# A decoder layer of attention, cross-attention and FFN on one core: the hand-written order of all five engines replaced, large weights fetched behind wq

## The chip, the core and the metric

The kernel runs on one core of a Trainium2 chip. The time is device microseconds (us) for one execution; three executions of the kernel before took 316.17, 318.11 and 319.19 us, so its median is 318.11 us. Lower is better.

## What is computed

16 sequences of 128 positions with 256 features go through three blocks. Each block is followed by a sum with its input and a layer norm without weights (`_layernorm`).

```python
# block 1: linear attention by a running sum
q, k, v = x @ Wq.T, x @ Wk.T, x @ Wv.T
x = ln(x + (q * cumsum(k * v, axis=-2) * denom) @ Wo.T)
# block 2: 32 query heads of 8 features on 8 key/value heads; keys = values = ctx_512 (16, 128, 64)
x = ln(x + softmax(x_heads @ ctx_heads.T / sqrt(8)) @ ctx_heads)
# block 3: FFN of 1024 with block quantisation over 32 values
xb = bf16(x);  h = bf16(ln(xb) * ln_w + ln_b)
h = bf16(mx_quant(h) @ mx_quant(W1).T + b1);  h = bf16(gelu(h))
h = bf16(mx_quant(h) @ mx_quant(W2).T + b2)
x = ln(x + bf16(xb + h))
```

`mx_quant` takes the largest magnitude of each 32 values, makes a power of two of it, divides, rounds and clips, and multiplies back.

## The kernel before

The 16 sequences are 8 pairs; all work is on pairs `p` = 0 to 7, with `b` = 0 or 1 for the sequence in the pair. Every engine has its own program: a `head()` that is written out, a `step(p, on)` that is repeated (`run_steps(step, 5, 9)`, four times, with `p[n]` = t - n, so that one step works on pair t-0 to t-6 in different stages), and a `tail()` written out. The engines meet only at semaphores. Each engine executes its list strictly in the order in which the calls stand, so that order is the schedule: an instruction that waits holds up all that stand behind it. The change rewrites these lists.

What each engine does, with the names used below:

- **SP** (SyncE) issues the DMAs: `load_xt` (L333 on, the transposed input), `load_x`, `load_keys`, `load_values`, `load_bias`, `load_weight(name)` for diag, wo, w1, ident, ln, tri, w2, and `store`. The ScalarE queue issues wkv (two halves) and wq at its start.
- **PE** (TensorE): `first_kv` and `kv_proj` (keys and values of block 1), `q_proj`, `running_sum` (product with a triangle), `out_proj`, `x1T` (transposes), `scores_a` (L2020, scores from which only the maximum is taken), `maxT`, `scores_b` (L2045, scores less the maximum, transposed), `weigh` (L2058), `values_back` (L2066), `weights_T`, `h_T`, `ffn_up` (L2097, L2099), `g_T` (L2111), `ffn_down` (L2122, L2124).
- **ACT** (ScalarE) copies most results out of the PSUM banks and computes `exps` (L835), `gelu` (L855), `norm1`, `norm2_x2`, `norm4`, `y2_copy` (L885), `hidden` (L849), `pv_copy` (L839). Going from Exp to Gelu and back loads a table.
- **DVE** (VectorE): `first_low`, `k_times_v` (L1220), `q_times_sum` (L1226), `residual1` (L1233), `moments` and `mean_var` (L1210, L1216), `maxima` (L1255, eight for each `p, b`, each over one `scores_a` result of 128x512), `max_high`, `max_low`, `denominators`, `attention`, `norm2`, `norm3`, and the quantisation in seven pieces: `quantise_weight(n, j, i)` for four parts of each of the two FFN weights, `quantise_h(p, i)` and `quantise_g(p, b, i)`, where i = 0 is the reduction (L1341) and 4 to 6 the wide products (L1350, L1352, L1354). For pair 7 the DVE also has `last_residual2`, `last_weight3`, `last_quantise_h` and so on, for one sequence at a time.
- **POOL** (GpSimd): `keys_rounded`, `keys` (L531), `split_xt_high` (L502), `split_xt_low` (L507), `split_bias(0..3)` (L449 to L462), `var_eps` (L481) and `rstd` (L486) of each norm, `shift_product`, `shift`, `split_x1_high`, `split_x1_low`, `residual2`, `weight3` (L568), `shift3` (L574), `ffn_out` (L580), `residual3` (L587).

The dependencies that matter below: `maxima(p,b,k)` waits for `scores_a(p,b,k)`; `scores_a` of k of 2 or more waits for the maximum two before it, since two banks are used in turn; `scores_b(p,b,k)` waits for the exponential two before it; `q_proj(p,0)` waits for `k_times_v(p,0)`; `quantise_h(p,0)` waits for POOL's `shift3(p)`, and this for DVE's `norm3`; `ffn_up` of pair 7 needs `last_quantise_h(b,6)` by way of `h_T(7,b)`; `g_T(p,b)` needs all seven pieces of `quantise_g(p,b)`.

`warm(bk, n)`, a filler of matmuls on zeros, is defined in the kernel before and called nowhere.

## Time and profile before

| | us |
|---|---|
| median of three executions | 318.11 |
| lowest, highest | 316.17, 319.19 |
| the profiled execution | 319.24 |
| its span, first to last instruction | 317.4 |
| outside the span | 1.8 |
| DVE busy in the span | 270.3 (85%) |
| PE busy | 263.5 (83%) |
| ACT busy | 223.3 (70%) |
| POOL busy | 182.8 (58%) |
| mean granted TensorE clock | 0.92 |

Times inside the profile count from the first instruction of the span. The span falls into a head up to 101.6 us, four repeated steps up to 222.7 us (found by the DVE's `maxima`, which recur every 30.2 to 30.5 us) and a tail. A row of the timeline gives start, duration, engine, line, operation, output<-input, a count where several were merged, and in brackets the idle time before it with what ended it.

### The profile page before, as it was taken

The numbers are of one execution on the slowest core, as the hardware profiler recorded it, in microseconds if no ns is written. First come the engines' busy times: TensorE is split into PE (matmuls) and PEld (weight loads), VectorE is DVE, ScalarE is ACT, GpSimd is POOL, SyncE is SP. The second block draws the span as 40 slices with busy tenths as digits, with TensorE's granted clock in tenths as the row PEclk, the third lists the DMA queues.
The fourth block names the chain that finished last, engine by engine and source line by source line (L and its number), as shares of the span: only waits on it lengthen the run. The fifth ranks groups of instructions, "written<-read, shape, count | busy, mean of one in ns | idle before, by whom it ended". The sixth has DMA issues, their size and how long they took to land. (4 is left out here: it accounts for less than half of the span.)

```text
span 317.4 us, 5160 instructions
## 1 busy us (share of the span) xinstructions
PE 263.5 (83%) x1575; PEld 164.7 (52%) x1584; DVE 270.3 (85%) x665; ACT 223.3 (70%) x364; POOL 182.8 (58%) x255
## 2 busy tenths in 40 slices
...
DMA packets 10066, 12.28 MB, mean 39 GB/s; under 512 B 2995, under 2 KB 7347, under 8 KB 9782
## 3 DMA queue, kind: packets, MB, share of 16 engines
...
q8 instruction: 13, 0.21, 0.3%
...
## 5 line engine op out<-in xcount | busy, mean ns | idle before, releaser
L1255 DVE TENSOR_REDUCE nm<-bank 128x4 f32<-128x512 f32 x128 | 84.3, 677 | 8.6 <-PE bank L2020 8.4
L835 ACT ACTIVATE p_sb<-bank 128x512 f32<-128x512 f32 x128 | 73.3, 597 | 8.9 <-PE bank L2045 7.7
L2020 PE MATMUL bank<-kbd,xT 96*128 96x512 f32 x128 | 57.6, 468 | 5.1 <-ACT xT L811 3.4
L2045 PE MATMUL bank<-xT,kbd 104*128 104x512 f32 x128 | 58.1, 466 | 4.0 <-ACT p_sb L835 2.4
L481 POOL TENSOR_SCALAR ve<-mv 128x2 f32<-128x2 f32 (+1 forms) x36 | 8.0, 221 | 63.4 <-DVE mv L1216 62.3
L531 POOL TENSOR_TENSOR kbd<-k3r,diag_sb 96x512 fp32r<-96x512 f32 x32 | 33.1, 1047 | 7.3 <-PE bank L2045 6.8
L2020 PEld LDWEIGHTS bank<-kbd,xT 96*128 96x128 f32 x128 | 25.1, 197 | 22.8 <-DVE nm L1255 12.3
L2045 PEld LDWEIGHTS bank<-xT,kbd 104*128 104x128 f32 x128 | 24.9, 196 | 21.1 <-ACT p_sb L835 14.1
L1341 DVE TENSOR_REDUCE am<-g_sb 128x32 f32<-128x1024 bf16 x16 | 30.2, 1891 | 5.2 <-ACT g_sb L855 5.2
L2058 PE MATMUL bank<-p_sb,va_sb 128*32 128x512 f32 x256 | 34.5, 631 | 0.0
L486 POOL TENSOR_TENSOR rs<-ve,nhalf 128x2 f32<-128x2 f32 (+1 forms) x36 | 27.1, 755 | 2.4
L859 ACT ACTIVATE gT<-bank 128x1024 bf16<-128x1024 bf16 x16 | 16.5, 1029 | 16.4 <-PE bank L2111 16.3
L1941 PE MATMUL bank<-wkv_r,xt_r 128*128 128x512 f32 x84 | 26.8, 452 | 0.0
L811 ACT ACTIVATE xT<-bank 96x512 fp32r<-96x512 f32 x32 | 18.9, 590 | 9.0 <-PE bank L2004 8.9
L2111 PE MATMUL bank<-idb,gq 128*128 128x128 bf16 x128 | 12.2, 252 | 14.6 <-DVE gq L1354 14.6
L849 ACT ACTIVATE y_sb<-bank 128x512 bf16<-128x512 f32 x32 | 18.9, 595 | 4.3 <-PE bank L2099 3.2
L828 ACT ACTIVATE xT<-bank 8x1024 fp32r<-8x1024 bf16 x16 | 16.2, 1015 | 6.0 <-PE bank L2033 5.5
L2124 PE MATMUL bank<-w2T,gT 128*128 128x256 bf16 x128 | 19.7, 305 | 0.0
L1210 DVE BATCH_NORM_STATS2 st<-r_sb 128x6 f32<-128x256 f32 x48 | 19.3, 415 | 0.2
L2111 PEld LDWEIGHTS bank<-idb,gq 128*128 128x128 bf16 x128 | 9.0, 113 | 19.8 <-DVE gq L1354 17.3
L1941 PEld LDWEIGHTS bank<-wkv_r,xt_r 128*128 128x128 f32 x84 | 17.1, 214 | 3.7 <-issue 0.2
L2004 PE MATMUL bank<-idr,x 128*96 128x128 f32 x128 | 17.0, 255 | 1.8 <-ACT xT L828 1.4
...
## 6 DMA issues: line engine op xcount, KB each, us to landing
xt_sb<-in_xt SPq DMA_DIRECT2D x8, 256.0 KB, 3.2
x_sb<-in_x SPq DMA_DIRECT2D x8, 256.0 KB, 3.0
out_dram<-o_sb SPq DMA_DIRECT2D x7, 256.0 KB, 2.2
...
x_all<-in_w SPq DMA_DIRECT2D x1, 1024.0 KB, 8.3
w_raw<-in_w SPq DMA_DIRECT2D x1, 1024.0 KB, 7.8
p_sb<-in_wkv ACTq DMA_DIRECT2D x2, 256.0 KB, 3.8
...
```

What stands on the lines that cost most here:

```text
L486: gp.tensor_tensor(rs[:, part(b)], ve[:, part(b)], nhalf[:, part(b)], ALU.pow).then_inc(rs_ready, batches(b))
L531: gp.tensor_tensor(kbd[0:MR, b, u, :, :], k3r[:, b, u, :].bitcast(F32).unsqueeze(1).to_broadcast([MR, KU, P]), diag_sb[0:MR, :].unsqueeze( ...
L835: sc.activation(p_sb[:, k, :], bankB[k % 2][:, :], ACT.Exp, scale=SCORE_SCALE).then_inc(s_ex, 1)
L1210: ve.bn_stats(st[:, b, :], rows).then_inc(st_ready, 1)
L1255: ve.tensor_reduce(nm[:, b, u, g, :], bankA[(2 + k + 11 * b) % 2][:, :].rearrange("p (k t) -> p k t", k=KU), AX.X, ALU.max, negate=True).t ...
L1341: last = ve.tensor_reduce(am, h.rearrange("p n i k -> p n k i"), AX.X, ALU.max, apply_absolute_value=True)
L1941: last = mm(bankP[b][:, :], xt_r[:, a, c, b, :], wkv_r[:, w, c, :], start=c == 0 and n == 0, stop=c == KC - 1 and n == len(PARTS) - 1)
L2020: mm(bankA[(2 + k + 11 * b) % 2][:, :], xT[0:MR, b, u, g, :], kbd[0:MR, b, u, :, :].rearrange("r k t -> r (k t)"), start=True, stop=True). ...
L2045: mm(bankB[k % 2][:, :], kbd[0:MR + 2 * KU, b, u, kk, :], xT[0:MR + 2 * KU, b, u, :, :].rearrange("r g s -> r (g s)"), start=True, stop=Tr ...
L2058: last = mm(value_bank(p, b)[VW * k:VW * (k + 1), :], va_sb[:, at0:at0 + VW], p_sb[:, u * KU + k, :], start=u == 0, stop=u == U - 1, tile_ ...
L2111: last = tp(dst[:, c, :], gq[:, b, c * P:(c + 1) * P], idb[:, :])
L2124: last = mm(dst, gT[:, b, c, :], w2T[:, c, :], start=False, stop=c == FC - 1)
```

## The change

No arithmetic is added or removed. All `head`, `step` and `tail` lists of SP, PE, ACT, DVE and POOL are written in a new order. Besides this:

```diff
 # load_weight, SP
+                if name in ("w1", "w2", "ln"):
+                    sp.wait_ge(s_w["wq"], 16)
                 sp.dma_start(dst, src).then_inc(s_w[name], 16)
 # split_xt_high, POOL
                 if later(p):
                     pool.wait_ge(s_qp, KC * p)
+                    pool.wait_ge(s_kvp, PB * p)
 # ffn_down, PE
-                if p == LAST:
-                    last.then_inc(s_f2, 1)
-                elif b == PB - 1:
-                    last.then_inc(s_f2, PB)
+                last.then_inc(s_f2, 1)
 # new, called nowhere
+            def warm_last(n):
+                pe.wait_ge(s_ex, 16 * NP)
+                for _ in range(n):
+                    mm(bankB[0][:, :], zero_b[:, 0:P], zero_b[:, :], start=True, stop=True)
```

So w1, w2 (1 MB each) and ln are issued only when wq has landed. The middle one fits an order in which a query projection may end before the last key/value projection. The third counts each `ffn_down` alone, so that they may stand in either order. No filler is called in either kernel.

**SP, the first loads.** Before:

```order
L340 DMA xt_sb<-in_xt 128x512
L370 DMA diag_sb<-in_diag 128x4
L370 DMA wo_sb<-in_wo 128x512
L370 DMA x_all<-in_w 128x2048
L362 DMA bias_f<-in_bias 1x1280 [waits setup_zeroed]
L362 DMA bias_f<-in_bias 1x1280 x2
L352 DMA k_sb<-in_ctx 96x512
L340 DMA xt_sb<-in_xt 128x512 [waits first_low_parts]
L357 DMA cv_sb<-in_ctxv 128x2x64
```

and now (`x_all<-in_w` is w1, `w_raw<-in_w` is w2):

```order
L340 DMA xt_sb<-in_xt 128x512
L362 DMA bias_f<-in_bias 1x1280 [waits setup_zeroed]
L362 DMA bias_f<-in_bias 1x1280 x2
L357 DMA cv_sb<-in_ctxv 128x2x64
L352 DMA k_sb<-in_ctx 96x512
L372 DMA diag_sb<-in_diag 128x4
L372 DMA tri_sb<-in_tri 128x128
L372 DMA wo_sb<-in_wo 128x512
L372 DMA x_all<-in_w 128x2048 [waits loaded_wq]
L372 DMA w_raw<-in_w 128x2048 [waits loaded_wq]
L340 DMA xt_sb<-in_xt 128x512 [waits first_low_parts]
```

The bias, the keys and the triangle moved ahead of w1, and w2 moved ahead of the second `load_xt`, of the identity and of `load_x(0)`.

**DVE, from the gelu quantisation of pair 6 to the statistics of pair 7, sequence 1.** Before, the second `attention(7,1,..)` and what follows it (`st<-r_sb` is `moments(7,1)`, the first of the chain that ends in the second FFN input of pair 7):

```order
L1282 TENSOR_TENSOR att<-bank,rden 128x4x4x8
L1350 TENSOR_TENSOR gz<-g_sb,in 128x1024
L1299 TENSOR_TENSOR r_sb<-x_all,att 128x256
L1341 TENSOR_REDUCE am<-g_sb 128x32
L1352 TENSOR_SCALAR gz<-gz 128x1024
L1344 TENSOR_SCALAR am<-am 128x32
L1346 TENSOR_SCALAR sc<-am 128x32
L1354 TENSOR_TENSOR gq<-gz,sc 128x1024
L1348 TENSOR_SCALAR in<-sc 128x32
L1350 TENSOR_TENSOR gz<-g_sb,in 128x1024
L1210 BN_STATS st<-r_sb 128x6
```

and now, where `h_sb` with 128x8 results is `last_quantise_h(0,..)`:

```order
L1279 TENSOR_TENSOR att<-bank,rden 128x4x4x8 x2
L1341 TENSOR_SCALAR am<-am 128x32
L1345 TENSOR_SCALAR in<-sc 128x8
L1296 TENSOR_TENSOR r_sb<-x_all,att 128x256
L1347 TENSOR_TENSOR z<-h_sb,in 128x256
L1207 BN_STATS st<-r_sb 128x6
L1213 BN_AGGR mv<-st 128x2
L1343 TENSOR_SCALAR sc<-am 128x32
L1338 TENSOR_REDUCE am<-g_sb 128x32
```

The statistics moved ahead of the second reduction of pair 6, and the FFN input of pair 7, sequence 0, is quantised in between.

**PE, the last FFNs.** Before, after the up-projections of pair 6 (`idb,gq` is `g_T`, `w2T,gT` `ffn_down`, `idb,hq` `h_T`, `w1T,hT` `ffn_up`):

```order
L2111 MATMUL bank<-idb,gq 128x128 x16
L2122 MATMUL bank<-bias_h,ones_b 128x256
L2124 MATMUL bank<-w2T,gT 128x256 x8
L2122 MATMUL bank<-bias_h,ones_b 128x256
L2124 MATMUL bank<-w2T,gT 128x256 x8
L2081 MATMUL bank<-idb,hq 128x128 x4
L2097 MATMUL bank<-bias_h,ones_b 128x512
L2099 MATMUL bank<-w1T,hT 128x512 x2
```

and now:

```order
L2081 MATMUL bank<-idb,hq 128x128 x2
L2097 MATMUL bank<-bias_h,ones_b 128x512
L2099 MATMUL bank<-w1T,hT 128x512 x2
L2111 MATMUL bank<-idb,gq 128x128 x8
L2097 MATMUL bank<-bias_h,ones_b 128x512
L2099 MATMUL bank<-w1T,hT 128x512 x2
L2111 MATMUL bank<-idb,gq 128x128 x8
L2122 MATMUL bank<-bias_h,ones_b 128x256
L2124 MATMUL bank<-w2T,gT 128x256 x8
L2081 MATMUL bank<-idb,hq 128x128 x2
L2122 MATMUL bank<-bias_h,ones_b 128x256
L2124 MATMUL bank<-w2T,gT 128x256 x8
```

Sequence 0 of pair 7 is projected up before pair 6 is projected down; sequence 1 follows between the two down-projections.

Other moves that are spoken of below, as lines of the diff:

```diff
 # POOL head
+                split_bias(0)
+                split_bias(1)
                 keys_rounded(0)
...
 # DVE head
                 first_low(3)
+                k_times_v(0, 0)
                 quantise_weight(0, 3, 0)
...
 # PE step: the first calls now
+                    kv_proj(p[1], 0, 0)
+                    kv_proj(p[1], 0, 1)
+                    scores_b(p[3], 0, 0)
+                    scores_b(p[3], 0, 1)
+                    x1T(p[3], 1, 1)
+                    kv_proj(p[1], 1, 0)
+                    q_proj(p[1], 0)
+                    kv_proj(p[1], 1, 1)
                     scores_b(p[3], 0, 2)
                     scores_a(p[3], 1, 0)
...
 # PE tail: the scores of pair 6 now end ahead of weigh(6, 0, 0)
+                scores_a(6, 1, 6)
+                scores_a(6, 1, 7)
                 scores_b(6, 0, 6)
                 scores_b(6, 0, 7)
+                g_T(4, 1)
                 weigh(6, 0, 0)
...
 # PE tail: and those of pair 7, sequence 0, ahead of weigh(6, 1, 0)
+                scores_a(7, 0, 6)
+                scores_a(7, 0, 7)
+                ffn_up(5, 1, 0)
+                weigh(6, 1, 0)
...
 # ACT tail
                 maxT(7, 1)
+                norm2_x2(6, 0)
+                norm2_x2(6, 1)
+                exps(7, 1, 0)
                 y2_copy(5)
-                exps(7, 1, 0)
...
 # POOL tail
+                ffn_out(5)
                 var_eps(7, mv2, ve2, s_mv2, s_ve2, 0)
                 rstd(7, ve2, rs2, s_ve2, s_rs2, 0)
+                residual3(5)
                 var_eps(7, mv3, ve3, s_mv3, s_ve3, 0)
-                ffn_out(5)
-                residual3(5)
                 rstd(7, ve3, rs3, s_ve3, s_rs3, 0)
```

## Rows read from the trace of the kernel before

**Rows 1.** The page's first part: busy time of the two busiest engines.

```profile
PE 263.5 (83%) x1575; PEld 164.7 (52%) x1584; DVE 270.3 (85%) x665; ACT 223.3 (70%) x364; POOL 182.8 (58%) x255
```

**Rows 2.** By stretch: length, busy PE, PEld, DVE, ACT, POOL, clock, DMA share, GB/s.

```profile
28.20:60.00 31.80, 27.52 (x148) 19.02 (x149) 30.01 (x68) 14.13 (x27) 20.74 (x23) 0.95 0.11 32
60.00:101.60 41.60, 38.69 (x240) 23.26 (x239) 37.69 (x93) 33.42 (x54) 28.49 (x36) 1.00 0.13 40
...
162.30:192.50 30.20, 29.15 (x196) 19.01 (x195) 28.91 (x72) 27.59 (x46) 21.81 (x31) 1.00 0.13 36
...
222.70:246.90 24.20, 22.58 (x116) 11.62 (x117) 16.97 (x41) 17.86 (x33) 14.57 (x18) 0.80 0.03 12
246.90:266.30 19.40, 14.83 (x83) 7.45 (x83) 17.96 (x44) 17.00 (x25) 8.33 (x14) 0.91 0.04 14
...
280.40:293.70 13.30, 6.48 (x36) 4.16 (x36) 12.02 (x39) 2.70 (x4) 3.38 (x8) 0.50 0.00 1
293.70:317.40 23.70, 9.79 (x47) 5.53 (x48) 11.68 (x29) 10.00 (x17) 5.09 (x10) 0.64 0.10 35
```

**Rows 3.** Timeline of the DVE, head: first reductions, stalls, first maximum.

```profile
10.40 3.04 DVE L1341 TENSOR_REDUCE wam<-x_all 128x16 f32<-128x512 f32 x3 [1.65 <-DMA x_all<-in_w]
...
15.24 2.42 DVE L1346 TENSOR_SCALAR wsc<-wam 128x16 bf16<-128x16 f32 x1
...
20.33 0.17 DVE L1346 TENSOR_SCALAR wsc<-wam 128x16 bf16<-128x16 f32 x1
...
24.93 0.42 DVE L1220 TENSOR_TENSOR kv_sb<-bank,v_sb 128x256 f32<-128x256 f32 x1 [1.36 <-ACT v_sb L816]
...
28.23 0.69 DVE L1255 TENSOR_REDUCE nm<-bank 128x4 f32<-128x512 f32 x1
```

**Rows 4.** Timeline of POOL, head.

```profile
15.15 1.26 POOL L449 TENSOR_SCALAR bias_h<-bias_f 96x1280 bf16<-96x1280 f32 x1
16.37 1.26 POOL L507 TENSOR_TENSOR xt_r<-xt_sb,xt_r 128x512 fp32r<-128x512 f32 x1
...
29.33 2.62 POOL L451 TENSOR_TENSOR bias_rest<-bias_f,bias_h 96x1280 f32<-96x1280 f32 x1
```

**Rows 5.** DMA issues: size, median us from issue to landing.

```profile
x_all<-in_w SPq DMA_DIRECT2D x1, 1024.0 KB, 8.3
...
p_sb<-in_wq ACTq DMA_DIRECT2D x1, 256.0 KB, 5.7
```

**Rows 6.** Timeline of the DVE, tail: the waits, and one late statistic.

```profile
231.23 0.69 DVE L1255 TENSOR_REDUCE nm<-bank 128x4 f32<-128x512 f32 x1 [1.48 <-PE bank L2020]
...
237.00 0.69 DVE L1341 TENSOR_REDUCE am<-h_sb 128x16 f32<-128x512 bf16 x1 [2.78 <-POOL h_sb L574]
...
245.27 0.69 DVE L1255 TENSOR_REDUCE nm<-bank 128x4 f32<-128x512 f32 x1 [1.12 <-PE bank L2020]
...
276.42 0.41 DVE L1293 TENSOR_SCALAR h_sb<-xb_all,mv,rs 128x256 f32<-128x256 bf16 x1 [3.44 <-POOL rs L486]
...
280.82 0.41 DVE L1299 TENSOR_TENSOR r_sb<-x_all,att 128x256 f32<-128x256 f32 x1
...
284.96 0.42 DVE L1210 BATCH_NORM_STATS2 st<-r_sb 128x6 f32<-128x256 f32 x1
...
298.93 1.87 DVE L1341 TENSOR_REDUCE am<-g_sb 128x32 f32<-128x1024 bf16 x1 [5.20 <-ACT g_sb L855]
```

**Rows 7.** Timeline of PE, tail: one `weigh`, the last `g_T` and `ffn_down`.

```profile
228.53 1.94 PE L2058 MATMUL bank<-p_sb,va_sb 128*32 128x512 f32 x8
...
232.47 1.07 PE L2058 MATMUL bank<-p_sb,va_sb 128*32 128x512 f32 x8
...
290.81 1.91 PE L2124 MATMUL bank<-w2T,gT 128*128 128x256 bf16 x8
...
306.95 1.04 PE L2111 MATMUL bank<-idb,gq 128*128 128x128 bf16 x8 [0.23 <-DVE gq L1354]
```

**Rows 8.** Timeline of ACT: issue of wq, and both `norm2_x2(6)` where they stood.

```profile
1.64 0.45 ACTq L779 DMA_DIRECT2D p_sb<-in_wq  x1
...
262.91 1.08 ACT L869 ACTIVATE x_all<-r_sb,nb,rs 128x256 f32<-128x256 f32 x2
```

More of the change, by code:

```diff
@@ L1030, in step @@
                 if on[4]:
-                    hidden(p[4], 0, 0)
-                    norm2_x2(p[4], 1)
+                    hidden(p[4], 0, 1)
                 if on[3]:
@@ new lines, in head @@
+                moments(1, 1, r1_sb[:, 1, :], st1, s_r1, 2 * 1 + 2, s_st1)
+                maxima(0, 1, 0)
+                quantise_weight(1, 0, 3)
+                quantise_weight(1, 2, 3)
+                quantise_weight(1, 1, 1)
+                quantise_weight(1, 3, 3)
+                maxima(0, 1, 1)
+                mean_var(1, 1, st1, mv1, s_st1, s_mv1)
+                maxima(0, 1, 2)
+                k_times_v(2, 0)
+                maxima(0, 1, 3)
+                quantise_weight(0, 0, 3)
@@ new lines, in head @@
+                quantise_weight(1, 1, 4)
+                moments(0, 0, r2_sb[:, 0, :], st2, s_r2, 2 * 0 + 1, s_st2)
+                moments(0, 1, r2_sb[:, 1, :], st2, s_r2, 2 * 0 + 2, s_st2)
+                maxima(1, 1, 0)
+                mean_var(0, 0, st2, mv2, s_st2, s_mv2)
+                maxima(1, 1, 1)
+                maxima(1, 1, 2)
+                mean_var(0, 1, st2, mv2, s_st2, s_mv2)
+                quantise_weight(1, 3, 5)
+                quantise_weight(1, 1, 5)
+                k_times_v(3, 1)
@@ new lines, in tail @@
+                quantise_g(6, 0, 0)
+                denominators(7, 1)
+                attention(7, 1, 0)
+                attention(7, 1, 1)
+                quantise_g(6, 0, 1)
+                last_quantise_h(0, 3)
+                last_residual2(1)
+                last_quantise_h(0, 4)
+                moments(7, 1, r2_sb[:, 1, :], st2, s_r2, 2 * 7 + 2, s_st2)
+                mean_var(7, 1, st2, mv2, s_st2, s_mv2)
+                quantise_g(6, 0, 2)
+                quantise_g(6, 1, 0)
@@ L2341, in step @@
                 if on[3]:
[L2342 removed]
                     scores_a(p[3], 1, 7)
+                    weigh(p[3], 0, 1)
                 if on[5]:
```

1027 lines of the change are left out of this document (483 added, 544 removed).

## Prediction
> **What bounds the kernel now.** I read the page's busy times first. DVE is busy 270.3 of 317.4 us and PE 263.5 [rows 1], so neither is hidden behind another engine and DVE leaves 47.1 us idle in all. No instruction is added or removed on either, so a new order can only buy idle time back or make more of it. The reader should therefore look for where those 47 us lie, and the table by stretch shows it [rows 2]. In one repeated step DVE is busy 28.91 of 30.20 us and PE 29.15: 1.3 and 1.05 us free. From 28.2 to 60.0 us DVE has 1.8 us free, from 60.0 to 101.6 us 3.9. In the tail it is different: 24.20 - 16.97 = 7.2 us free up to 246.9, 1.4 up to 266.3, 1.3 from 280.4 to 293.7 and 23.70 - 11.68 = 12.0 at the end. Then I read the timeline of the DVE at the two ends for what ended each wait [rows 3, 6], and that of POOL, PE and ACT beside it [rows 4, 7, 8]. So the middle is bound by DVE's own work with PE close behind, and the ends by waits. Times are worked out against the profiled execution: 319.24 us, a span of 317.4 and 1.8 around it. It lies 1.1 us above the median of 318.11, and I take that off at the end.
>
> **Head, up to the first maximum.** DVE starts the first `maxima` at 28.23 us. Before it stand three losses [rows 3]: 1.65 us until w1 lands, 2.42 us for a tiny scalar piece that elsewhere takes 0.17 (so 2.25 lost), and 1.36 us until a copy of ACT. The long piece lies exactly over POOL's `split_bias(0)` and `split_xt_low(1)`, which run from 15.15 to 17.63 us, and ends at 17.66 [rows 4].
> The new order issues bias and keys first, so POOL can do both bias splits before 10 us; nothing small of the DVE stands there any more, and I count the 2.25 us as gone. The 1.36 us wait goes too: `kv_proj(1)` waited on PE behind `out_proj(0,1)`, which comes earlier since `k_times_v(0,0)` no longer stands behind three weight reductions (3.04 us).
> Against this stands the new wait for wq. wq was issued at 1.64 us [rows 8] and took 5.7 us [rows 5], so it landed at 7.3; w1 took 8.3 from its issue, sharing the queues. If both stay as slow, w1 lands at 7.3 + 8.3 = 15.6 us, 5.2 later than before, and all DVE reductions with it. The other bound is no delay at all: the same megabytes move, wq no longer shares with w1, and w1 no longer with wkv. I take w1 at 11 us, 0.6 late, nearer the second bound, since total bytes bind; `k_times_v(0,0)` is done meanwhile. Queued behind the waiting DMA on SP are w2, the second `xt`, the identity and x(0); the identity is used late, the others I expect by 15 us, before their users. So -2.25 - 1.36 + 0.6 = -3.0, and 0.5 less for what is late next (q and running sum on PE): **-2.5 us**, between -4.5 and +2.
>
> What could spoil it is that POOL's bias splits, 1.26 and 2.62 us long [rows 4], now run while DVE makes the low parts of wkv and wq, on which the first projections wait. Rows 3 and 4 show one DVE instruction held until POOL is done, but of another kind.
> The Trainium skill, "SBUF — State Buffer", section "Who interferes with whom", says that a vector instruction with two SBUF inputs contends with a GpSimd one that reads SBUF, and that the one that starts first has the shared ports for its whole length. By that rule those subtractions would be held as well, and this part of the change speaks against itself; the held piece agrees with the exclusive lock, and no row here shows it for a subtraction.
>
> **Steps and the later head, 28.2 to 222.7 us.** The order of PE at the start of a step now puts all of `kv_proj` and `q_proj(p,0)` ahead of `scores_a(p,1,0)`. Is it late? From the last `maxT` on, 8 + 12 + 6 + 3 + 4 = 33 matmuls stand ahead of it (19 before). At 29.15/196 = 0.149 us each [rows 2] that is 4.9 us (2.8). DVE now has 18 instructions between `max_low(p,0)` and `maxima(p,1,0)` (12 before), at 28.91/72 = 0.40 us each 7.2 us (4.8). So the margin is 2.3 us against 2.0: still hidden. The same holds for POOL's `weight3` and `shift3`, whose place in the chain is the same, so their short wait stays. DVE work is equal, so a step cannot fall under 28.9 us: at most -1.3 us for each of four steps, and I see nothing that would add more than 1. I take **+0.5 us** for the whole stretch, for small waits in the 42 + 32 us of head with its weight pieces in another order; bounds -5 and +5. If the margin is used up, every further us on PE costs one per step.
>
> **Tail, by the waits of rows 6.**
> - `scores_a(6,1,6)` and `(6,1,7)` stood behind `weigh(6,0,0)`, which took 1.94 us there against 1.07 at the other clock [rows 7]; DVE waited 1.48 us. They now stand ahead: -1.5.
> - `scores_a(7,0,6)` and the next stood behind `weigh(6,1,..)`; DVE waited 1.12 us at 245.27. Now ahead: -1.0.
> - The wait of 2.78 us at 237.00 for POOL stays: `quantise_h(5)` has nothing new before it.
> - ACT now does both `norm2_x2(6)`, 1.08 us [rows 8], between `maxT(7,1)` and the exponentials of the last sequence, where they used to fill a gap; with `y2_copy` behind two split down-projections I count +1.3.
> - POOL no longer has `residual3(5)` in front of `rstd` of sequence 0 of pair 7, so most of the 3.44 us wait at 276.42 goes. That by itself buys nothing, since the second sequence still waits for its exponentials; it makes room to quantise sequence 0 early. 0.
> - From the end of `attention(7,1)` to the last `last_quantise_h`, DVE has 39 instructions in 13.30 us, 12.02 busy, 0.31 each [rows 2]; `moments(7,1)` came 284.96 - 281.23 = 3.7 us after its input [rows 6]. Now 34 stand there and the statistics follow at once: 5 x 0.31 = 1.5, less 0.4 for a chain with less between its links: -1.1.
> - The end. DVE waited 5.20 us for the gelu and then did both quantisations, 298.93 to 306.95 us [rows 6, 7], 8.0 us or 4.0 each. Now sequence 0 is quantised in the gap. The gelu of sequence 1 stays about 7.4 us behind `last_quantise_h(1,6)`: it loses the wait for sequence 0 and gains `ffn_down(6,1)`, 1.91 us [rows 7]. Then 4.0 us: `g_T(7,1)` can start 11.5 us after 293.7 instead of 13.2. `ffn_down(7,0)` is no longer behind `g_T(7,1)`, worth 0.2 more: -1.9. Cover gone: if `ffn_down(6,1)` delays the gelu by all of its 1.91 us, this term is 0.
>
> Tail: -1.5 - 1.0 + 1.3 - 1.1 - 1.9 = **-4.2 us**, between -8 and +1.
>
> **Sum.** -2.5 + 0.5 - 4.2 = -6.2 us: 313.0 on the scale of the profiled execution, **311.9 us** as a median.
>
> **Rivals.**
> 1. *The ends give little.* w1 comes 3 us late or POOL holds the low parts by its 1.26 + 2.62 us, and `ffn_down(6,1)` takes the last term away. Head +1 instead of -2.5, tail -2.3: 318.1 + 1 + 0.5 - 2.3 = 317.3; with the tail part alone 313.8, with the head part alone 315.4. For it: neither the landing nor such a hold is in the trace. Against it: 12 us of free DVE at the end are there to be used.
> 2. *More is won.* If the steps give back half of their 1.3 us and the 7.2 us of the first tail stretch are halved, that is another -2.6 - 1.1: 308. For it: the free time is there. Against it: in the steps PE is nearly full as well.
> 3. *Slower: the granted clock.* PE has 1.05 us free per step, at clock 1.00. Where `kv_proj` and `q_proj` are missing, the clock was 0.80 over a stretch [rows 2] and `weigh` took 1.94 instead of 1.07 us. `q_proj(p,0)` now stands early and waits for `k_times_v(p,0)`, with the scores behind it; if these pauses let the clock fall, PE decides from 29.15/30.2 = 0.965 down. At 0.90 a step takes 32.4 us, 2.2 more, over some 5.4 steps (162.7 us from 60.0 to 222.7) 11.9: 323.8 us. Against it: all steps before ran at 1.00 with pauses of their own, and the matmuls are as many.
> That the change does not do what it says is no rival: the order on each engine is fixed by the lists.
>
> **How the numbers follow.** My forecast 0.52, rival 1 0.22, rival 2 0.11, rival 3 and unseen waits in the steps 0.15. About 1% (3.2 us) is what a measurement of this kernel can tell from no change. The forecast and rival 2 are faster by more, 0.63; of rival 1 most lies within 1%, with a little of rival 3: 0.21; the rest, 0.16, slower. The range takes in rival 2's side (307.0) and, upward, rival 1 and the beginning of rival 3 (319.5).
>
> **What would show it.** Right: the first `maxima` at 25 to 26.5 us, no scalar piece of 2.4 us near 15 us, step length 29.8 to 30.5 us by the distance of equal `maxima`, clock 1.00 in the steps, the wait of 5.20 us before the first gelu reduction of pair 7 split into two short ones, and 22 us instead of 23.7 from the last `last_quantise_h` to the end. Wrong: `first_low` pieces of more than 1 us beside a bias split, w1 reductions that begin after 12 us, or steps over 31 us with PE waiting ahead of `q_proj`.

## The result, and the profile after

The changed kernel took 329.17 us (median of four executions, 327.76 to 330.04), the kernel before 318.65 us beside it on the same chip: ratio 1.033, interval 1.026 to 1.041. It is slower by 10.5 us, where I had forecast 6.2 us faster; the time lies outside my range as well. The profiled execution after took 330.04 us with a span of 328.2. In the ratios of this document executions more than 1.5% above the fastest of their kernel are left out; in e3_tail (below) one execution of 311.86 us stands so far under the other three (316.72 to 319.11) that no ratio is left.

The page of the changed kernel, busy times and granted clock (one digit per 8.2 us, in tenths of full speed):

```profile
PE 270.9 (83%) x1584; PEld 169.9 (52%) x1584; DVE 277.3 (85%) x665; ACT 221.5 (67%) x364; POOL 184.8 (56%) x255
...
PEclk9987799879999999999999999999568985895675
```

DVE does the same 665 instructions as in [rows 1] and is busy 7.0 us longer, PE 7.4 us. So the loss is not only waiting, of which the DVE has 3.8 us more (50.9 for 47.1): the same instructions took longer. To find where, I cut both spans at the same work: the first `maxima`, and then `max_high(p,b)`, which closes the eight maxima of a sequence. Both tables by stretch have the columns length, busy PE, PEld, DVE, ACT, POOL, clock, DMA share, GB/s. Cuts: first maximum, `max_high(0,0)`, `(1,1)`, `(2,1)`, `(6,0)`, end. The kernel before:

```profile
28.20:36.40 8.20, 5.87 (x23) 3.76 (x23) 8.17 (x16) 0.51 (x2) 6.97 (x8) 1.00 0.03 5
36.40:77.80 41.40, 38.35 (x224) 25.18 (x224) 37.98 (x93) 26.54 (x47) 28.30 (x35) 0.96 0.14 43
77.80:111.40 33.60, 31.67 (x212) 20.28 (x217) 31.25 (x77) 28.79 (x47) 20.53 (x28) 1.00 0.08 25
111.40:216.80 105.40, 102.22 (x678) 66.15 (x675) 100.65 (x243) 96.06 (x157) 79.08 (x107) 1.00 0.10 29
216.80:317.40 100.60, 67.94 (x371) 35.72 (x372) 73.56 (x198) 64.43 (x101) 37.64 (x61) 0.78 0.04 14
```

and after:

```profile
26.30:38.10 11.80, 9.80 (x29) 6.47 (x29) 9.73 (x14) 0.00 (x0) 6.11 (x6) 0.71 0.02 3
38.10:85.70 47.60, 38.78 (x225) 25.28 (x225) 41.63 (x102) 25.58 (x46) 26.94 (x33) 0.93 0.13 39
85.70:119.10 33.40, 30.58 (x204) 18.72 (x201) 30.36 (x71) 28.76 (x46) 20.35 (x27) 1.00 0.09 25
119.10:226.40 107.30, 102.96 (x688) 67.55 (x684) 100.85 (x243) 94.90 (x158) 77.49 (x105) 1.00 0.09 28
226.40:328.20 101.80, 72.23 (x375) 38.93 (x373) 76.66 (x199) 64.89 (x102) 38.32 (x64) 0.72 0.04 14
```

The account: up to the first maximum -1.9; to `max_high(0,0)` +3.6; to `(1,1)` +6.2; to `(2,1)` -0.2; the steps +1.9; the tail +1.2. The sum is +10.8, the difference of the spans. Nine tenths of it lie between 26 and 86 us, in the stretch for which I had allowed half a microsecond. Of the 6.2, 3.65 are busy time of the DVE. This is the DVE there, after:

```profile
54.19 0.28 DVE L1349 TENSOR_SCALAR wqb<-wz 128x512 bf16<-128x512 int16 x1
...
55.00 3.39 DVE L1349 TENSOR_SCALAR wqb<-wz 128x512 bf16<-128x512 int16 x2
...
58.91 1.22 DVE L1343 TENSOR_SCALAR wsc<-wam 128x16 bf16<-128x16 f32 x1
60.04 0.68 DVE L1252 TENSOR_REDUCE nm<-bank 128x4 f32<-128x512 f32 x1
60.64 1.02 DVE L1349 TENSOR_SCALAR wqb<-wz 128x512 bf16<-128x512 int16 x1
```

and POOL in the same microseconds, `split_bias(3)`:

```profile
55.57 2.67 POOL L456 TENSOR_TENSOR bias_low<-bias_rest,bias_mid 96x1280 bf16<-96x1280 f32 x1
58.40 1.71 POOL L460 TENSOR_SCALAR bias_h<-bias_mid 32x1280 bf16<-32x1280 bf16 x1 [0.16 <-POOL bias_low L456]
60.26 1.25 POOL L463 TENSOR_SCALAR bias_h<-bias_low 32x1280 bf16<-32x1280 bf16 x1 [0.15 <-POOL bias_h L460]
```

A cast takes 0.28 us when alone and two take 3.39 beside `bias_low`; each long piece ends within 0.2 us of the end of POOL's instruction. I call such a piece held. The maximum at 60.04, which reads a PSUM bank, keeps its 0.68. Adding up what pieces took over their usual time, where that is more than 0.3 us, the stretch from `max_high(0,0)` to `(1,1)` has 3.3 us of it before and 6.9 after. Between the first maximum and `max_high(0,0)` there is none before, and after there are three, which usually take 0.69, 0.17 and 0.17 us, 2.4 over in all:

```profile
26.90 1.27 DVE L1347 TENSOR_TENSOR wz<-x_all,win 128x512 int16<-128x512 f32 x1
28.10 1.00 DVE L1341 TENSOR_SCALAR wam<-wam 128x16 uint32<-128x16 uint32 x1
...
31.79 1.14 DVE L1341 TENSOR_SCALAR wam<-wam 128x16 uint32<-128x16 uint32 x1
```

And PE from 28 us on, after:

```profile
29.75 1.39 PE L2020 MATMUL bank<-kbd,xT 96*128 96x512 f32 x2 [1.32 <-DVE nm L1252]
31.33 0.80 PE L2020 MATMUL bank<-kbd,xT 96*128 96x512 f32 x1 [0.19 <-DVE nm L1252]
31.93 3.78 PE L1980 MATMUL bank<-wo_sb,vh_sb 128*128 128x256 f32 x8
```

`out_proj(1)` took 1.99 us before. PE had paused 1.32 us (28.43 to 29.75) for a maximum that stood behind two held pieces; the granted clock was 1.00 up to 29.4 us and at its lower level from there to 36.3 (0.50 from 31 to 35 us, where the kernel before has 1.00); and `residual1(1)`, now ahead of two maxima, waited 1.77 us for the product.

### The profile page after: what moved, and what is told of

It reads as the page before. It is cut to its first block, busy times and chain, and to the rows that moved or that the text cites. A ratio compares the mean times of both kernels' runs of the same rounds, so it can differ in the third digit from the quotient of the medians.

```text
span 328.2 us, 5176 instructions
## 1 busy us (share of the span) xinstructions
PE 270.9 (83%) x1584; PEld 169.9 (52%) x1584; DVE 277.3 (85%) x665; ACT 221.5 (67%) x364; POOL 184.8 (56%) x255
## 3 DMA queue, kind: packets, MB, share of 16 engines
q1 hardware_dynamic: 9606, 11.16, 10.5%
## 4 chain that ended last, share of the span: by engine, by line
PE 42%; DVE 34%; issue 10%; ACT 8%; DMA 3%; POOL 2%; ACTq 0%; POOLq 0%; DVEq 0%
DVE nm L1252 7%; PE bank L2020 7%; PE bank L2058 6%; PE bank L2045 5%; DVE am L1338 5%; PE bank L1980 5%; PE bank L2124 4%; PE bank L2099 3%; DVE st L1207 3%; DVE gz L1347 2%; PE bank L1941 2%; DVE xb_all L1285 2%; PE bank L2097 2%; DVE gq L1351 2%; DMA x_all<-in_w 2%
## 5 line engine op out<-in xcount | busy, mean ns | idle before, releaser
L835 ACT ACTIVATE p_sb<-bank 128x512 f32<-128x512 f32 x128 | 72.1, 602 | 22.2 <-PE bank L2045 21.5
L2020 PE MATMUL bank<-kbd,xT 96*128 96x512 f32 x128 | 63.2, 514 | 12.3 <-DVE nm L1252 7.8
L2045 PE MATMUL bank<-xT,kbd 104*128 104x512 f32 x128 | 55.2, 467 | 7.4 <-ACT p_sb L835 5.3
L533 POOL TENSOR_TENSOR kbd<-k3r,diag_sb 96x512 fp32r<-96x512 f32 x32 | 33.6, 1066 | 23.7 <-PE bank L2045 23.6
L2020 PEld LDWEIGHTS bank<-kbd,xT 96*128 96x128 f32 x128 | 26.8, 210 | 34.8 <-DVE nm L1252 21.6
L2058 PE MATMUL bank<-p_sb,va_sb 128*32 128x512 f32 x256 | 35.3, 648 | 0.0
L1338 DVE TENSOR_REDUCE am<-g_sb 128x32 f32<-128x1024 bf16 x16 | 30.5, 1906 | 3.0 <-ACT g_sb L855 3.0
L1941 PE MATMUL bank<-wkv_r,xt_r 128*128 128x512 f32 x84 | 26.0, 431 | 0.0
L859 ACT ACTIVATE gT<-bank 128x1024 bf16<-128x1024 bf16 x16 | 16.4, 1024 | 10.8 <-PE bank L2111 10.8
L1980 PE MATMUL bank<-wo_sb,vh_sb 128*128 128x256 f32 x64 | 19.5, 439 | 0.6 <-DVE vh_sb L1223 0.6
L2099 PE MATMUL bank<-w1T,hT 128*128 128x512 bf16 x64 | 20.0, 395 | 0.0
L582 POOL TENSOR_TENSOR s_sb<-y_sb,xb_all 128x512 bf16<-128x512 bf16 x7 | 8.1, 1156 | 18.2 <-ACT y_sb L885 18.2
L1941 PEld LDWEIGHTS bank<-wkv_r,xt_r 128*128 128x128 f32 x84 | 16.3, 208 | 3.1 <-issue 0.3
```

The costliest lines, as they stand in the source:

```text
L533: gp.tensor_tensor(kbd[0:MR, b, u, :, :], k3r[:, b, u, :].bitcast(F32).unsqueeze(1).to_broadcast([MR, KU, P]), diag_sb[0:MR, :].unsqueeze( ...
L835: sc.activation(p_sb[:, k, :], bankB[k % 2][:, :], ACT.Exp, scale=SCORE_SCALE).then_inc(s_ex, 1)
L1338: last = ve.tensor_reduce(am, h.rearrange("p n i k -> p n k i"), AX.X, ALU.max, apply_absolute_value=True)
L1941: last = mm(bankP[b][:, :], xt_r[:, a, c, b, :], wkv_r[:, w, c, :], start=c == 0 and n == 0, stop=c == KC - 1 and n == len(PARTS) - 1)
L1980: last = mm(out_bank(p, b)[:, b * D:(b + 1) * D], vh_sb[:, e, b, :], wo_sb[:, e, :], start=e == 0, stop=e == KC - 1)
L2020: mm(bankA[(2 + k + 11 * b) % 2][:, :], xT[0:MR, b, u, g, :], kbd[0:MR, b, u, :, :].rearrange("r k t -> r (k t)"), start=True, stop=True). ...
```

## The experiments

In the mixed kernels a part (head, step or tail) is taken on all engines from one kernel and the rest from the other. Where only one order is mixed in, the last 11 to 24 calls of each head belong to the step, since the two orders can't be joined elsewhere; such a seam costs something of its own, which I give. Ratios are to the kernel before, on the same chip. The table holds, from one profiled execution each, the lengths of the account above: A first maximum to `max_high(0,0)`, B to `(1,1)`, C to `(2,1)`, step (mean of three, `(3,0)` to `(6,0)`), tail (`(6,0)` to the end).

| kernel | span | A | B | C | step | tail | ratio, interval |
|---|---|---|---|---|---|---|---|
| before | 317.4 | 8.1 | 41.5 | 33.5 | 30.21 | 100.6 | |
| after | 328.2 | 11.8 | 47.6 | 33.4 | 30.82 | 101.8 | 1.033, 1.026 to 1.041 |
| e1_head | 326.8 | 11.6 | 46.6 | 36.6 | 30.28 | 101.5 | 1.037, 1.029 to 1.045 |
| e2_step | 324.7 | 8.1 | 41.5 | 35.6 | 30.83 | 103.5 | 1.023, 1.011 to 1.036 |
| e3_tail | 316.5 | 8.1 | 41.5 | 33.6 | 30.30 | 99.0 | see there |
| e4_loads | 319.4 | 8.1 | 41.5 | 33.6 | 30.29 | 100.8 | 1.006, 1.001 to 1.011 |
| e5_step_qcopy | 323.0 | 8.1 | 41.5 | 35.5 | 30.75 | 103.6 | 1.025, 1.019 to 1.030 |
| e6_tail_mix | 314.7 | 8.1 | 40.7 | 33.6 | 30.31 | 98.4 | 0.992, 0.987 to 0.997 |
| e7_head_bias_early | 323.7 | 12.0 | 43.2 | 36.6 | 30.31 | 100.7 | 1.025, 1.021 to 1.030 |
| e8_head_pieces_late | 324.5 | 11.4 | 44.6 | 36.4 | 30.30 | 100.7 | 1.028, 1.021 to 1.036 |
| e9_head_three | 327.0 | 12.2 | 44.8 | 36.5 | 30.28 | 100.8 | 1.035, 1.029 to 1.042 |
| e10_step_pool | 325.4 | 8.1 | 41.5 | 35.1 | 30.82 | 103.7 | 1.024, 1.019 to 1.030 |
| e11_head_filler | 326.9 | 9.7 | 46.7 | 36.6 | 30.29 | 100.9 | 1.035, 1.028 to 1.042 |
| e12_best | 321.4 | 10.2 | 40.0 | 33.6 | 30.28 | 101.0 | 1.012, 1.006 to 1.018 |
| e13_step_two | 326.8 | 8.1 | 40.6 | 38.9 | 30.48 | 103.2 | 1.014, 1.006 to 1.023 |
| e14_filler_first | 324.0 | 9.7 | 46.6 | 36.4 | 30.30 | 100.6 | 1.028, 1.020 to 1.037 |
| e15_head_first_pieces | 328.7 | 12.5 | 43.4 | 37.8 | 30.29 | 102.0 | 1.025, 1.013 to 1.037 |
| e16_after_four | 319.4 | 11.9 | 43.2 | 33.4 | 30.46 | 99.1 | 1.010, 1.005 to 1.015 |

The profiled executions of e13 and e15 were the longest of their four, so their spans lie higher than their ratios. A of the old head is 8.1 in all eight kernels that have it, and the old step 30.2 to 30.3, so 0.2 us can be read in these. B of the old head is 41.5 in six kernels and 40.6 and 40.7 in e13 and e6, where the clock was 1.00 all through it for 0.96 in the others, so in B only more than 1 us can be read. The start of the first maximum can't be read from one pair: it lies between 27.3 and 29.8 us in the seven kernels with the old lists up to there and between 24.9 and 27.4 in the nine with the new ones, 28.5 and 26.0 on average. Nor can the tail: the same new tail took 101.8 in the changed kernel and 99.0 and 99.1 in e3 and e16, at different clocks, told below.

**One part alone.** e1, e2, e3: one of head, step, tail is new. e4: the SP's head list and the wait for wq are new.

```diff
 # e4
+                if name in ("w1", "w2", "ln"):
+                    sp.wait_ge(s_w["wq"], 16)
```

> The kernel before with the new head of all engines (with the wait for wq), its own repeated step and tail; the last 11 to 24 calls of each head, which prepare the first step, stay as in the kernel before. Theory A (the loss was made in the head after the first maximum, where the DVE's weight pieces and POOL's bias pieces now stand otherwise): first maximum near 26.3 us, maxima(2,1,1) near 110 us instead of 103.4, steps of 30.2 us, median 7 to 8 us over the kernel before, ratio 1.02 to 1.025. Theory B (the whole order is denser, the granted clock falls by its total and each part alone costs little): maxima(2,1,1) within 2 us of 103.4 and a ratio under 1.01.

> The kernel before with the new repeated step alone (and the last calls of each head, which prepare it). Theory A: each of the four steps 0.6 us longer because of its own order: 30.8 instead of 30.2 us between equal maxima, median +2.4 us, ratio about 1.008. Theory B: the longer steps were a consequence of the state in which the new head left the engines: 30.2 us per step, ratio 1.00.

> The kernel before with the new tail alone. By my prediction's tail sum -4.2 us (ratio 0.987). By what the changed kernel's milestones say (+1.4 from maxima(6,1,1) to the last maximum, -0.6 after it): +0.8 us, ratio 1.003. Theory B (the clock of 0.71 to 0.76 in that stretch instead of 0.83 to 0.90 was left over from the slower steps before): then the tail alone shows 0.83 to 0.90 again and gains 2 us or more, ratio 0.994 or less.

> The kernel before with the new order of the SP's loads and the wait for wq alone, all other lists as before. Theory A (loads do no harm): w1 reductions of the DVE start at 11 to 12 us instead of 10.40, first maximum at 28.2 to 29.5, ratio 0.998 to 1.004. Rival (the loads bring w2, x or the second xt late and so cause the later loss): maxima(2,1,1) 3 us or more after 103.4 and ratio 1.01 or more.

The head alone is as slow as the whole change (329.48 us against 319.51). It starts the first maximum at 24.9 us, the earliest of all, and loses that and much more in A and B. Its C, 3.1 too long, is the seam: in the changed kernel C is no longer than before. Theory B of e1, that only the whole is slow, has fallen. The step alone is 0.62 us longer per step, as in the changed kernel; e2's seam costs 2.1 in C. Its tail is 2.9 longer, but 1.9 of that lies between `max_high(7,0)` and `(7,1)` at a clock of 0.65 for 0.90, and the same list took as long there (19.0 to 19.3 us) in e1, e11 and e15: that part is the clock and not the seam. e3: medians 317.51 against 319.51 us, a gain of 1.6 in the tail by the table, less than the 4.2 I had summed and more than the changed kernel shows. Between `max_high(6,1)` and `(7,1)` its clock was 0.97 and 0.83, where the changed kernel had 0.80 and 0.75, which is theory B's way. e4: the loads change no later length, so they are not the loss. Its first maximum is at 29.7 us, but e10, with the old loads, has 29.8, so a delay by the loads isn't shown.

**The head: held pieces.** e7 moves one POOL call into a gap of 10.9 us, e8 moves DVE pieces (and `attention(0,0,1)` behind `maxima(1,0,1)`), e9 does both and one thing more.

```diff
 # e7, POOL head
                 split_bias(2)
+                split_bias(3)
...
                 split_xt_low(3)
-                split_bias(3)
```

```diff
 # e8, DVE head; e9: this, e7 and residual1(1) behind maxima(0,0,7)
-                quantise_weight(1, 3, 4)
-                quantise_weight(1, 1, 2)
                 maxima(1, 0, 0)
-                quantise_weight(1, 0, 5)
-                quantise_weight(0, 1, 6)
...
                 maxima(1, 0, 4)
+                quantise_weight(1, 3, 4)
+                quantise_weight(1, 1, 2)
                 maxima(1, 0, 5)
+                quantise_weight(1, 0, 5)
                 maxima(1, 0, 6)
+                quantise_weight(0, 1, 6)
```

> As e1_head, with one edit: POOL's split_bias(3) (bias_low 2.66 us, then 1.71 and 1.25) stands right behind split_bias(2), where POOL idles 10.9 us from 31.5 us on, and no longer beside the weight pieces of the DVE at 54 to 60 us. Theory A1 (these pieces were held by POOL: two of 0.28 us took 3.38, one of 0.17 took 1.23, one of 0.28 took 1.02, 4.6 us in all): the held pieces vanish there, and the median falls by 3 to 5 us under e1_head. Theory A2 (the order of the DVE starves PE, the held pieces are a detail): they vanish, but the median falls by less than 1.5 us.

> As e1_head, with one edit: four weight pieces of the DVE that stood between max_low(0,1) and maxima(1,0,1) stand behind maxima(1,0,4) to (1,0,6), and the second half of attention(0,0) behind maxima(1,0,1). Theory A2 (PE waits for maxima held back by weight pieces, its clock falls to half, and the rest of the head runs late): maxima(1,0,1) 2 us or more earlier, clock in 50 to 70 us above the 0.81 of e1_head, median 3 us or more under e1_head. Theory A1: the pieces held by POOL only move; median within 1.5 us of e1_head.

> As e1_head, with three edits together: the bias edit of e7, the four weight pieces of e8, and residual1(1) behind maxima(0,0,7) again, as in the kernel before. Spans so far: e1_head 326.8, e7 323.7, e8 324.5. If the held pieces and the starved PE are two separate losses: span near 320.5 (326.8 - 3.1 - 2.3 - 1 for the residual's wait), max_high(2,0) near 98 us, median ratio 1.01. If both edits attack the same microseconds (the DVE's stretch from 53 to 60 us): span 323 or more, no better than e7 alone.

The same pieces of the DVE in e7:

```profile
54.41 0.96 DVE L1358 TENSOR_SCALAR wqb<-wz 128x512 bf16<-128x512 int16 x2
55.30 0.68 DVE L1356 TENSOR_TENSOR wz<-w_raw,win 128x512 int16<-128x512 f32 x1
55.90 0.16 DVE L1352 TENSOR_SCALAR wsc<-wam 128x16 bf16<-128x16 f32 x1
58.04 0.69 DVE L1261 TENSOR_REDUCE nm<-bank 128x4 f32<-128x512 f32 x1 [1.98 <-PE bank L2033]
```

0.96 for 3.39 and 0.16 for 1.22 us. B falls by 3.4 us. The median falls by 3.3, from 10.0 to 8.0 us over that of the kernel before on the same chip, and the ratio from 1.037 to 1.025: theory A1, at the low end of its range or below it. The clock is not what e7 gained: e11, without this edit, had the same mean clock in B (0.96) and took 46.7. The gain is not larger, since of the 4.2 us freed here (2.43, 1.06 and, at 60.64, 0.74) 1.98 come back as a wait for PE. e8 gains 2.0 in B, between the two theories, but e9 with both is no better than e8 and no better than e7 (44.8, 44.6 and 43.2). A separate loss by a starved PE, as A2 said, should have shown in e9 on top of e7's gain, and it did not: that theory has no support left. Where e8's 2.0 come from is open. Its two casts beside `bias_low` still take 3.39 us, and the moved pieces are held again where they stand now (1.09 us for two of 0.17, 1.12 for one of 0.28); its clock in B was 1.00 for e1's 0.93. Putting `residual1(1)` back bought nothing while `out_proj(1)` still ran slow (A 12.2).

**The head: the clock.** e11 and e14 put matmuls on zeros, whose results are thrown away, into pauses of PE.

```diff
 # e11, PE head
+                warm(bankB[0], 8)
                 maxT(0, 1)
 # e14, PE head
+                warm(bankB[0], 2)
                 scores_a(0, 0, 2)
                 running_sum(1)
+                warm(bankB[0], 5)
                 scores_a(0, 0, 3)
                 scores_a(0, 0, 4)
+                warm(bankB[0], 1)
                 scores_a(0, 0, 5)
+                warm(bankB[0], 1)
                 out_proj(1, 0)
```

> As e1_head, with eight matmuls of zeros on PE ahead of maxT(0,1), where it idles 2.45 us (they are thrown away). The granted clock was 0.81 from 50.5 to 68.8 us in e1_head. Theory clock (the pause lets TensorE's clock fall and this sets the time after it): the matmuls after 52.8 us run at full speed, clock 0.9 or more there, max_high(1,0) 1.5 us or more earlier than 68.8, median lower by as much. Theory A (the DVE's pieces are the bound there): PE is faster, but max_high(1,0) moves by less than 0.5 us.

> As e1_head, with nine matmuls of zeros on PE between scores_a(0,0,2) and out_proj(1), in pauses of 0.35 to 1.22 us (thrown away). In all kernels with the new head the granted clock is 0.50 somewhere between 27 and 35 us, where the kernel before has 1.00, and out_proj(1) takes 3.5 to 3.6 us instead of 1.99. Theory clock: with the pauses filled the clock stays at 1.00, out_proj(1) takes 2.0 us, max_high(0,0) comes 1.5 to 2 us earlier counted from the first maximum (9.7 instead of 11.6), and the median falls by 1 to 2 us. Theory A: out_proj is faster, but the DVE's held pieces still set max_high(0,0): under 0.7 us.

PE in e14, with the fillers from L1918:

```profile
26.94 1.24 PE L1918 MATMUL bank<-zero_b 128*128 128x512 bf16 x5
28.41 1.09 PE L2033 MATMUL bank<-kbd,xT 96*128 96x512 f32 x2 [0.23 <-DVE nm L1261]
29.34 0.39 PE L1918 MATMUL bank<-zero_b 128*128 128x512 bf16 x1
29.70 0.50 PE L2033 MATMUL bank<-kbd,xT 96*128 96x512 f32 x1
30.04 0.39 PE L1918 MATMUL bank<-zero_b 128*128 128x512 bf16 x1
30.30 1.99 PE L1993 MATMUL bank<-wo_sb,vh_sb 128*128 128x256 f32 x8
```

`out_proj(1)` takes 1.99 us again, the clock is 1.00 from 27 to 35 us, and A falls from 11.6 to 9.7, just the 1.9 that the clock theory said. The median is 2.3 us under e1's, but the intervals of the ratios overlap. In e11 the clock of the filler's stretch was 0.91 for 0.81 and B did not move (46.7): there the held pieces set the pace and a faster PE waits. But e11's A is 9.7 too, with no filler there: its clock stayed at 1.00 from 27 to 35 us after a pause of PE of 1.31 us. And in e1 the clock was at its lower level from 26.8 us on, before the pause of 1.22 us at 27.18. So what is shown is the price of the lower clock, 1.9 us in A and nothing in B of this head. That the pauses bring it on and that the fillers keep it off is not shown: without them it stayed up once (e11) and fell five times (the changed kernel, e1, e7, e8, e9), with them it stayed up in the one profile there is.

> As e7_head_bias_early, with one more edit on the DVE: the two weight pieces between maxima(0,0,0) and maxima(0,0,1), which were held by POOL (1.27 for 0.91 and 1.00 for 0.17 us), stand behind maxima(0,0,3). Theory A: PE's pause there goes, its clock stays up, max_high(0,0) 10 us or less after the first maximum instead of 12.0, median 1.5 to 2.5 us under e7. Rival: the pieces are needed by something else at once or are held where they stand now: within 0.7 us of e7.

e15 is e7 with `quantise_weight(0,1,4)` and `(0,0,1)` behind `maxima(0,0,3)`. A is 12.5: the rival was right. Both are held again where they stand now (1.24 and 0.72 us), and `x_all<-r_sb` takes 1.77 instead of 0.41 us beside the moved `bias_low`. (That piece takes 1.77 us in e7 already.) A's other 1.6 us (9.7 against 8.1) fit the three held pieces shown above, 2.4 us over their usual time, but no run took them away, so that is argued.

**The step.** e5 and e13 change ScalarE's list, e10 takes POOL's step from the kernel before.

```diff
 # e5, ACT step; e13 does both
+                    q_copy(p[1])
                     pv_copy(p[3], 0)
-                    q_copy(p[1])
 # e13, ACT step
                     hidden(p[4], 0, 0)
+                    norm2_x2(p[4], 1)
...
                     hidden(p[4], 1, 1)
-                    norm2_x2(p[4], 1)
                     gelu(p[4], 1)
```

> As e2_step (new repeated step alone), with one edit: ScalarE's q_copy(p[1]) stands ahead of pv_copy(p[3], 0) again. Theory A (the step's own loss is that q_copy waits behind pv_copy for weigh, and the DVE's q_times_sum for q_copy: 0.83 to 0.93 us in each step of e2_step): the wait of the DVE for q_sb goes and a step is 30.0 to 30.2 us again, median 2.5 to 3.5 us under e2_step. Rival (PE's new order at the start of the step, with 33 matmuls ahead of scores_a(p,1,0), is the bound): the step stays at 30.8 us, DVE waits for scores or its busy time instead.

> As e5_step_qcopy, with POOL's repeated step as in the kernel before, so that the new step differs on SP, PE, ACT and DVE alone. Theory H (what is left of the step's loss are DVE pieces held by POOL: xb_all 0.71 instead of 0.41 us beside split_x1_low, a cast of 0.52 beside shift3; none in a step of the kernel before): they move or vanish, step 30.2 to 30.4 us, span 1 to 2 us under e5 (323.0). Rival (the DVE's and PE's own new order makes the step): 30.7 us as in e5, with a wait of the DVE for POOL or PE in their place.

> As e5_step_qcopy, with one more edit on ScalarE: norm2_x2(p[4], 1) stands ahead of the last exponentials again and no longer between the last hidden and the second gelu. The chain of e5 runs through that place in each step: PE's last ffn_up, hidden, norm2_x2 0.49 us, gelu, the DVE's reduction that waits for it, then the DVE and PE on to the next weigh. Theory C (this instruction on the chain is the rest of the step's loss): step 30.2 us, spans 2 us under e5 (323.0), ratio about 1.018. Rival (the DVE's and PE's own order is the bound): 30.7 to 30.8 us again.

In the changed kernel DVE waits 0.9 us per step for `q_copy`, which stands behind a copy that waits for `weigh`. The waits of the DVE in two steps of it:

```profile
DVE vh_sb L1223 <- ACT q_sb L820: 1.9, 2, 0.9
DVE am L1338 <- ACT g_sb L855: 0.4, 2, 0.2
```

e5 took most of the first away (0.4 us left in three steps for 2.5) and the step stayed at 30.75, so my theory A fell. Of these 2.1 us, 1.2 came back as a wait for POOL's `shift3`, and the DVE was busy 0.6 longer. The critical chain of e5 ran through ScalarE's last `hidden`, `norm2_x2` and the gelu to the second wait, hence e13. Its step is 30.48, 0.27 less, and e16 has the same. But the gain does not lie in that wait: it is 0.6 us in three steps of e5 and 0.8 in e13. The DVE is as long idle in three steps (4.2 us) and its busy time falls from 87.97 to 87.23. The one piece that differs by more than 0.1 us is a cast beside POOL's `split_x1_high`, once in each step. e5:

```profile
167.57 0.71 DVE L1286 TENSOR_SCALAR xb_all<-r_sb,mv,rs 128x256 bf16<-128x256 f32 x1
167.37 1.39 POOL L548 TENSOR_SCALAR x<-x_all 128x512 fp32r<-128x512 f32 x2 [1.35 <-issue]
```

and e13:

```profile
171.96 0.41 DVE L1286 TENSOR_SCALAR xb_all<-r_sb,mv,rs 128x256 bf16<-128x256 f32 x1
172.09 1.33 POOL L548 TENSOR_SCALAR x<-x_all 128x512 fp32r<-128x512 f32 x2 [1.69 <-issue]
```

In e5 and in the changed kernel POOL begins first and the piece takes 0.71 us; in e13 the piece begins first and takes its 0.41. So 0.3 us of each step was a held piece again, and that `norm2_x2` itself lay on the way is not shown. The rest, 0.2 to 0.3 per step, stays open. With POOL's old list (e10) other pieces of the DVE were held than in e5, and the step was no shorter.

**The tail, and a kernel that beats both.** e6: new order to the maxima of `(7,0)`, then the order before to the last exponentials, then the new end, with the old head and step. e12: the same tail, the old step, and the new head up to the first maximum.

> The kernel before with a mixed tail: the new order up to the maxima of sequence 0 of pair 7, the order before from there to the exponentials of sequence 1, the new one for the end. In e3_tail the first part gained 2.3 us, the middle lost 1.0 up to the last maximum and 1.8 more up to the last last_quantise_h (ScalarE's exponentials of the last sequence began 2.1 us later), the end gained 2.5. Theory A (losses and gains belong to those places and add up): span 4 us under the kernel before, ratio 0.985 to 0.990. Rival (the middle's loss is the price of the first part, by a lower granted clock after it): ratio as e3_tail, 0.993 to 1.00.

> The part of each list that gained, together: the new head up to the first maximum (with the wait for wq and the new loads), then the order of the kernel before for the rest of the head and the repeated step, then the mixed tail of e6_tail_mix. Where the parts add up: first maximum near 25.5 us and max_high(2,0) 2 to 3 us under 95.8, tail as in e6_tail_mix (span 314.7), so a span of 312, ratio 0.98 to 0.985. Rival (the early head leaves the DVE's weight pieces to be made up later): max_high(2,0) at 95 to 97 us and ratio 0.99 to 0.995, as e6_tail_mix.

e6 is a little faster than the kernel before, ratio 0.992 (0.987 to 0.997) by my rule; the medians of all executions are 316.89 and 318.20, ratio 0.996. It is faster than the changed kernel. Its tail is 98.4 against 100.6, half of what I expected, not clearly better than the 99.0 of the new tail whole, so its gain over that is not shown. e12 was a failure of my join: pieces of weight that the old order does before the first maximum, and the new one after it, came all ahead of it (first maximum at 30.9 us), and one of them was held for 2.19 us beside POOL's keys. So e12 says nothing for or against the early start as such. Its tail, the same lists as e6's, took 101.0.

**The causes taken out of the changed kernel.** e16: all new lists, with the edits of e7, e15, e5 and e13.

> The changed kernel itself (all new lists) with four edits: split_bias(3) behind split_bias(2), the two weight pieces of e15, q_copy ahead of pv_copy, and norm2_x2 of e13. If these are the causes of its loss: first maximum at 26 us as it was, max_high(1,1) 5 us earlier than 85.7, steps of 30.2 instead of 30.8 us, together 7 us under its 329.2: 322, ratio 1.01. If the seams of e1 and e2 had misled me: less than 3 us under it, ratio above 1.02.

By stretch, e16, with the cuts as above:

```profile
25.40:37.30 11.90, 8.49 (x29) 5.73 (x29) 10.90 (x14) 0.00 (x0) 10.92 (x9) 0.86 0.02 4
37.30:80.50 43.20, 37.17 (x225) 24.93 (x225) 37.81 (x101) 25.57 (x46) 21.04 (x31) 0.96 0.15 43
80.50:113.90 33.40, 30.60 (x204) 18.71 (x201) 30.39 (x71) 28.76 (x47) 20.35 (x27) 1.00 0.08 25
113.90:220.40 106.50, 103.05 (x688) 67.56 (x684) 101.16 (x243) 94.45 (x159) 77.52 (x105) 1.00 0.10 29
220.40:319.40 99.00, 69.59 (x375) 37.17 (x373) 76.64 (x199) 64.32 (x101) 38.69 (x63) 0.75 0.04 15
```

321.25 us, 7.9 under the changed kernel where 7 were expected, ratio 1.010. The road is not quite the expected one: B gives 4.4 and the steps 0.9; the start gives 0.9 and the tail 2.8, where no edit was made. There the lists are the same and the clock is not: between `max_high(6,1)` and `(7,0)` PE was at 0.80 in the changed kernel and 18.8 us passed, in e16 16.5 at a clock that fell once instead of twice. Why the second fall comes in one and not in the other, after the same pauses (1.7 and 1.1 to 1.2 us for copies of ScalarE), I can't say. So of the 10.8 us of loss the edits account for 5.3 (B and steps), and with the clock's 1.9 in A, read from e11 and e14, some 7 are named; the rest of A, 0.2 to 0.3 us per step and the clock in the tail are not accounted for by an edit.

## Why the prediction was wrong

- **Head, up to the first maximum (-2.5; measured -1.9, and -2.4 as the difference of the averages over all kernels with each head).** Right in its size: the first maximum came at 26.29 (forecast 25 to 26.5), the w1 reductions begin at 11.07 us, 0.67 later, and the held scalar piece at 15 us is gone. In its parts not all: of the wait of 1.36 us for ScalarE's copy 0.80 are left. And the sign of being wrong that I had named, a `first_low` piece of more than 1 us beside a bias split, did come. The same subtraction before, after, and POOL's `split_bias(0)` after:

```profile
8.06 0.69 DVE L1173 TENSOR_TENSOR wq_r<-p_sb,wq_r 128x512 fp32r<-128x512 f32 x1 [1.32 <-ACT wq_r L791]
...
6.66 1.74 DVE L1170 TENSOR_TENSOR wq_r<-p_sb,wq_r 128x512 fp32r<-128x512 f32 x1
...
6.27 1.59 POOL L450 TENSOR_SCALAR bias_h<-bias_f 96x1280 bf16<-96x1280 f32 x1 [3.57 <-DMA bias_f<-in_bias]
```

  It takes 1.73 to 1.74 us in all kernels with the new head and 0.69 in all with the old one, e4 with the new loads among them. The sum had nothing for these 1.05 us; I had put them into rival 1, with a chance of 0.22. The sum also ended at the first maximum, as if nothing after it could lose the gain: the next 12 us lost it. The early start was not bought by putting the DVE's work off. Without what its pieces took over their usual time, it had done 16.1 us of work at its first maximum before and 17.1 after.
- **"Steps and the later head", +0.5 (measured +9.6 from the first maximum up to `(2,1)`, +1.9 in the steps).** This is the step that failed. Behind it stands the premise of the prediction's first paragraph, that a new order can only buy idle time back or make more of it: the DVE was busy 7.0 us longer with the same instructions. For the later head I counted neither instructions nor neighbours and took "small waits"; the bounds of 5 us on each side were too narrow too. I had read the held piece in the profile [rows 3, 4], and asked of the bias splits only whether they would hold the low parts in the first 10 us. `split_bias(3)`, whose place in POOL's list did not change but whose neighbours on the DVE did, was not looked at: it cost 3.4 us (e7). The steps, outside my 29.8 to 30.5 us at 30.82, hold a piece of the same kind (0.3 us each).
- The rule of the Trainium skill that I cited there, "SBUF — State Buffer", section "Who interferes with whom", names more than I used. In my words: copies, casts and scalar instructions of the vector engine that can run in a two-port mode contend as well, reductions never, and the loser is blocked for the whole instruction. The trace agrees on all three: casts and scalar pieces were held until POOL's instruction ended, and the reduction of w2 at 24.64 us in the changed kernel, which reads SBUF beside POOL's `keys` at 24.66, kept its 1.03 us. Read against the new neighbours instead of the old ones, it would have shown the loss.
- **Rival 3, the granted clock.** It was priced in the steps, where the clock stayed at 1.00. It struck in the head, at `out_proj(1)`, for 1.9 us (A 11.6 in e1, 9.7 in e11 and e14), and again in the tail.
- **The step.** My margin for `scores_a(p,1,0)` (33 matmuls against 18 DVE instructions) held; the DVE no longer waits for scores there. What I left out is ScalarE, where two calls changed places: `q_copy`, now behind a copy that waits, is worth 0.1 per step at most (e5), and `norm2_x2` 0.27 (e13), by way of the held cast.
- **Tail, -4.2 (measured +1.2; the new tail with the old head and step -1.6).** The first term (-1.5, scores ahead of `weigh`) is there: 16.4 us between `(6,0)` and `(6,1)` became 14.2 in e3 and 14.0 in the changed kernel. The second (-1.0) did not come: 15.7 became 16.1 in e3. The cost of both `norm2_x2(6)` (+1.3) has the right sign and about the size: in e3 the exponentials begin 2.1 us later and `max_high(7,1)` comes 0.9 later after `(7,0)`, but the clock there was lower too (0.83 for 0.90), and no run separates the two. The end too: from the last `last_quantise_h` 21.2 us in e3 for 23.7 before, -2.5 for my -1.9, where the wait of 5.20 us for the gelu is one of 1.70 in the changed kernel. Wrong is -1.1 for `moments(7,1)` early: counted from `max_high(7,1)`, the end of that quantisation came 1.8 us later (29.1 for 27.3), as the last exponentials did.
- **The sum.** Two terms that I worked out (start and end) came within 0.6 us, the start in part by luck, since the sum had left out a hold of 1.05 us. The one I did not work out was more than twenty times off (+0.5 for 11.5). The chance of 0.15 for slower was put on a mechanism with the right name and the wrong place.
